# The experts' router: ranks summed by TensorE, and one lane comparison for each pick

## The reference, cut to what matters

```python
x = x + attn(layernorm(x)); x = x + xattn(layernorm(x), ctx); x = x + ffn(layernorm(x))
# ffn, xf = 2048 tokens x 256:
gates = softmax(xf @ gate_w)                       # 8 experts
topw, topi = top_k(gates, 2);  topw = topw / sum(topw)
combine = sum(topw[:, :, None] * one_hot(topi, 8), axis=1)
h = gelu(_ln(einsum('td,edh->teh', xf, w1) + b1, ln1_g, ln1_b))
y = einsum('teh,ehd->ted', h, w2) + b2
out = _ln(einsum('ted,te->td', y, combine) + xf, ln_g, ln_b)
```

## Time and profile before

| what | value |
|---|---|
| median of 3 runs | 1327.8 us (1324.22 to 1328.14) |
| the profiled execution: its time, its span | 1325.4 us, 1323.6 us |
| TensorE, VectorE, ScalarE, GpSimd busy | 91%, 73%, 47%, 24% of the span |
| mean granted TensorE clock | 0.972 of full speed |
| router, from VectorE's read of the logits to the first gather | 1079.81 to 1105.57 us |
| experts' loop and the sum behind it | 1105.57 us to the end |

### The profile page before, as it was taken

One profiled execution on the slowest core, in us unless ns is written; L12 is line 12 of the kernel. 1 busy time (PEld: TensorE's weight loads), 2 busy tenths in 40 slices (PEclk: granted clock), 3 DMA queues, 4 the chain that ended last, 5 costly groups with the idle time before them and its releaser, 6 DMA issues. The chain is left out here.

```text
span 1323.6 us, 19479 instructions
## 1 busy us (share of the span) xinstructions
PE 1206.1 (91%) x6678; PEld 734.0 (55%) x6679; DVE 972.5 (73%) x1757; ACT 622.8 (47%) x1169; POOL 321.6 (24%) x275
## 2 busy tenths in 40 slices
PE   6699999999999999969999999999999844999976
PEld 5377777887788778743333334334333232666654
DVE  3788868877887688687768777876889545677746
ACT  4233343333333333216667766776777721444432
POOL 1422235222522122112200210120000312566640
PEclk8899999999999999999999999999999986999999
DMA  7000015000400000013720570074050161111125
GB/s 260 0 7 1 1 43 106 1 1 0 75 1 1 0 1 1 1 54 56 151 37 7 96 144 0 7 131 85 1 195 1 48 158 46 60 60 63 61 82 159
DMA packets 61888, 72.99 MB, mean 55 GB/s; under 512 B 14336, under 2 KB 53376, under 8 KB 61168
## 3 DMA queue, kind: packets, MB, share of 16 engines
q1 hardware_dynamic: 55712, 59.46, 19.4%
q0 software_dynamic: 3792, 10.36, 2.5%
q10 hardware_dynamic: 2304, 2.10, 0.5%
HBM read 52.86 MB, written 18.78 MB: 54 GB/s over the span
## 5 line engine op out<-in xcount | busy, mean ns | idle before, releaser
L1512 ACT ACTIVATE pt<-pR 128x512 f32<-128x512 f32 x512 | 287.8, 600 | 102.1 <-PE pR L1399 95.9
L1607 DVE TENSOR_REDUCE neg_max<-pS 128x1 f32<-128x1024 f32 x240 | 288.1, 1220 | 63.5 <-PE pS L1377 62.0
L1399 PE MATMUL pR<-qs,ks 100*128 100x512 bf16 x512 | 187.8, 385 | 3.9 <-DVE qs L1582 2.4
L1377 PE MATMUL pS<-ks,qs 100*128 100x512 bf16 x480 | 144.9, 384 | 8.0 <-DVE neg_max L1607 6.3
L1411 PE MATMUL b_pO<-pt,b_v 128*32 128x512 f32 x1024 | 138.0, 611 | 2.3 <-ACT pt L1512 1.8
L1399 PEld LDWEIGHTS pR<-qs,ks 100*128 100x128 bf16 x512 | 49.2, 98 | 150.0 <-ACT pt L1512 44.8
L382 PE MATMUL pP<-w_feat,a_xT 128*128 128x512 f32 x256 | 123.4, 606 | 2.0 <-ACT a_xT L620 1.2
L268 POOL TENSOR_TENSOR kf<-kf,fsum 128x2048 f32<-128x2048 f32 x16 | 57.9, 3621 | 221.9 <-DVE fsum L772 221.9
L268 POOL TENSOR_TENSOR qs<-qs,fsum 128x2048 f32<-128x2048 f32 x16 | 58.8, 3674 | 150.6 <-DVE fsum L772 150.6
L440 PE MATMUL pO<-v,am 128*128 128x96 f32 x512 | 91.1, 275 | 0.0
L639 ACT COPY qfT<-pT 128x512 f32<-128x512 f32 x64 | 37.1, 580 | 108.9 <-PE pT L408 108.9
(11 more groups left out here) (321 smaller groups left out, 2190.2 us busy)
## 6 DMA issues: line engine op xcount, KB each, us to landing
ks<-k_scr SPq DMA_DIRECT2D x8, 768.0 KB
qs<-q_scr SPq DMA_DIRECT2D x24, 256.0 KB
k_scr<-f SPq DMA_DIRECT2D x18, 256.0 KB, 2.7
ks<-k_scr SPq DMA_DIRECT2D x8, 512.0 KB
ks<-in_L_ffn_w_dram SPq DMA_DIRECT2D x2, 2048.0 KB, 10.6
ks<-in_L_ffn_w_dram SPq DMA_DIRECT2D x4, 1024.0 KB, 9.6
c_y<-y_rows SPq DMA_DIRECT2D x16, 256.0 KB, 3.0
cx<-in_ctx_dram SPq DMA_DIRECT2D x3, 768.0 KB, 12.2
```

Source lines behind the costliest of these rows:

```text
L1377: ins = pe.matmul(pS1[:, slot, 512 * half:512 * half + 512], qs[0:KR, bass.ds(par, 1), h, P * t:P * t + P].rearrange("r a n -> r (a n)"), ...
L1399: pe.matmul(ring[bank], ks[0:KR, bass.ds(par, 1), h, P * j:P * j + P].rearrange("r a n -> r (a n)"), qs[0:KR, bass.ds(par, 1), h, :].rearr ...
L1512: nc.scalar.activation(pt[:, j % 2, i, :], ring[bank], ACT.Exp).then_inc(exp_done, 1)
L1607: nc.vector.tensor_reduce(neg_max[:, hg % 2, u // G, u % G:u % G + 1], pS1[:, u % 2, :], AX_X, ALU.max, negate=True).then_inc(max_done, 1)
```

## The change

- In the tail of the cross attention, two of the four `bn_stats` stand behind the first residual sum and two behind the second.
- `earlier` and `ones` get copies in bf16 (`earlier_h`, `ones_h`), cast by two more instructions ahead of the router; `both` and `lanes` become bf16. All hold whole numbers up to 127 (`both` 0 or 1).
- The copy of the logits goes; maximum and subtraction read them from PSUM.
- TensorE sums over tiles: sixteen matmuls of `ones_h` with 8 columns each, accumulated in `pT[1]`, give the totals of the experts; then one with `earlier_h` and fifteen with `ones_h`, over 120, 112, ... 8 columns, accumulated in `pT[0]`, give each tile's ranks with all earlier tiles in them. VectorE's copy and prefix sums go, and its three rank sums become one.
- `numbers` is formed ahead of `at_lane`, and `at_lane` by 32 instructions of 128 elements, each comparing the bf16 lanes with one number per partition. Each raises `hot_ready`, and each of TensorE's 32 matmuls waits for its own.
- The table of experts by slot is formed behind `from_now`.

```diff
--- before.py
+++ after.py
@@ -1726,9 +1726,10 @@
                 n = batch(B - 1, steps_before(B - 1), False, True, own)
                 for q, (kind, i, bank, _done) in enumerate(FINISH):
                     small(B - 1, kind, i, n + q, own, bank)
-                wait(dve, emptied, n + len(FINISH))
-                for t in range(T - TB, T):
-                    own.did(nc.vector.bn_stats(stats[:, t, :], xr[:, t, :]))
+                    if kind == "y":
+                        wait(dve, emptied, n + q + 1)
+                        for t in range(T - TB + 2 * i, T - TB + 2 * i + 2):
+                            own.did(nc.vector.bn_stats(stats[:, t, :], xr[:, t, :]))
 
 
 
@@ -1779,15 +1780,16 @@
         g2 = sb("g2", [P, T, E_])
         eq = sb("eq", [P, T, E_])
         sel = sb("sel", [P, 2, T, E_])
-        both = sb("both", [P, T, E_])
+        both = sb("both", [P, T, E_], BF16)
         rank = sb("rank", [P, T, E_])
-        tot = sb("tot", [P, 2, T, E_])
+        earlier_h = sb("earlier_h", [P, P], BF16)
+        ones_h = sb("ones_h", [P, P], BF16)
         order = sb("order", [P, E_])
         order_i = sb("order_i", [P, E_], I32)
         slot_i = sb("slot_i", [P, SLOTS], I32)
         slot = sb("slot", [P, SLOTS])
         lanes_i = sb("lanes_i", [P, P], I32)
-        lanes = sb("lanes", [P, P])
+        lanes = sb("lanes", [P, P], BF16)
         of_tile_i = sb("of_tile_i", [P, PICKS], I32)
         of_tile = sb("of_tile", [P, PICKS])
         of_lane_i = sb("of_lane_i", [P, PICKS], I32)
@@ -2012,13 +2014,20 @@
                     ins = pe.transpose(pH[1][:, P * c:P * c + P], lgT[:, P * c:P * c + P], ident[:, :])
                 ins.then_inc(lg_steps, 1)
                 pe.wait_ge(g_steps, 3)
-                pe.wait_ge(s_k, 7)
                 sel_2d = both[:, :, :].rearrange("p t e -> p (t e)")
-                pe.matmul(pT[0][:, 0:TE], earlier[:, :], sel_2d, start=True, stop=True).then_inc(rank_done, 1)
-                pe.matmul(pT[1][:, 0:TE], ones[:, :], sel_2d, start=True, stop=True).then_inc(rank_done, 1)
-
-                pe.wait_ge(hot_ready, 1)
+                for t in range(T):
+                    ins = pe.matmul(pT[1][:, 0:E_], ones_h[:, :], sel_2d[:, E_ * t:E_ * t + E_],
+                                    start=(t == 0), stop=(t == T - 1))
+                ins.then_inc(rank_done, 1)
+                pe.matmul(pT[0][:, 0:TE], earlier_h[:, :], sel_2d, start=True, stop=False)
+                for t in range(1, T):
+                    ins = pe.matmul(pT[0][:, E_ * t:TE], ones_h[:, :], sel_2d[:, 0:TE - E_ * t],
+                                    start=False, stop=(t == T - 1))
+                ins.then_inc(rank_done, 1)
+
+                pe.wait_ge(g_steps, 4)
                 for n in range(PICKS):
+                    wait(pe, hot_ready, n + 1)
                     ins = pe.matmul(pT[0][:, 0:2 * SLOTS], at_lane[:, n, :], numbers[:, n, :],
                                     start=(n == 0), stop=(n == PICKS - 1))
                 ins.then_inc(pairs_done, 1)
@@ -2182,16 +2191,16 @@
                 dve.wait_ge(s_k, 13)
                 own.did(nc.vector.tensor_copy(order[:, :], order_i[:, :]))
                 for to, what in ((slot, slot_i), (lanes, lanes_i), (of_tile, of_tile_i), (of_lane, of_lane_i),
-                                 (spare, spare_i)):
+                                 (spare, spare_i), (earlier_h, earlier), (ones_h, ones)):
                     own.did(nc.vector.tensor_copy(to[:, :], what[:, :]))
 
 
                 dve.wait_ge(lg_steps, 3)
-                did(nc.vector.tensor_copy(
-                    g1[:, :, :].rearrange("p (q c) e -> p c q e", q=B),
-                    pH[1][:, :].rearrange("p (c q e) -> p c q e", c=TB, q=B)[:, :, :, 0:E_]))
-                did(nc.vector.tensor_reduce(tmp[:, :], g1[:, :, :], AX_X, ALU.max))
-                nc.vector.tensor_tensor(g1[:, :, :], g1[:, :, :], tmp[:, :].unsqueeze(2).broadcast_to([P, T, E_]),
+                logits = pH[1][:, :].rearrange("p (c q e) -> p q c e", c=TB, q=B)[:, :, :, 0:E_]
+                tmp_4d = tmp[:, :].rearrange("p (q c) -> p q c", q=B)
+                did(nc.vector.tensor_reduce(tmp_4d, logits, AX_X, ALU.max))
+                nc.vector.tensor_tensor(g1[:, :, :].rearrange("p (q c) e -> p q c e", q=B), logits,
+                                        tmp_4d.unsqueeze(3).broadcast_to([P, B, TB, E_]),
                                         ALU.subtract).then_inc(g_steps, 1)
                 dve.wait_ge(g_steps, 2)
 
@@ -2217,17 +2226,8 @@
                 own.did(nc.vector.tensor_tensor(top[:, :, :], top[:, :, :],
                                                 tmp[:, :].unsqueeze(1).broadcast_to([P, 2, T]), ALU.mult))
 
-                dve.wait_ge(rank_done, 2)
-                did(nc.vector.tensor_copy(tot[:, 0].rearrange("p t e -> p (t e)"), pT[1][:, 0:TE]))
-                cur = 0
-                for step in (1, 2, 4, 8):
-                    nc.vector.tensor_copy(tot[:, 1 - cur, 0:step, :], tot[:, cur, 0:step, :])
-                    did(nc.vector.tensor_tensor(tot[:, 1 - cur, step:T, :], tot[:, cur, step:T, :],
-                                                tot[:, cur, 0:T - step, :], ALU.add))
-                    cur = 1 - cur
-                total = tot[:, cur]
-
-                did(nc.vector.tensor_scalar(tiles_i[:, :], total[:, T - 1, :], float(P - 1), None, ALU.add))
+                dve.wait_ge(rank_done, 1)
+                did(nc.vector.tensor_scalar(tiles_i[:, :], pT[1][:, 0:E_], float(P - 1), None, ALU.add))
                 did(nc.vector.tensor_scalar(tiles_i[:, :], tiles_i[:, :], 7, None, ALU.logical_shift_right))
                 own.did(nc.vector.tensor_copy(n_e[:, :], tiles_i[:, :]))
                 did(nc.vector.tensor_copy(ends[:, 0, :], tiles_i[:, :]))
@@ -2241,11 +2241,9 @@
 
                 did(nc.vector.tensor_tensor(y_base[:, :], end, n_e[:, :], ALU.subtract))
                 did(nc.vector.tensor_scalar(y_base[:, :], y_base[:, :], float(P), None, ALU.mult))
-                own.did(nc.vector.tensor_tensor(rank[:, 0, :], pT[0][:, 0:E_], y_base[:, :], ALU.add))
-                did(nc.vector.tensor_tensor(rank[:, 1:T, :].rearrange("p t e -> p (t e)"), pT[0][:, E_:TE],
-                                            total[:, 0:T - 1, :].rearrange("p t e -> p (t e)"), ALU.add))
-                did(nc.vector.tensor_tensor(rank[:, 1:T, :], rank[:, 1:T, :],
-                                            y_base[:, :].unsqueeze(1).broadcast_to([P, T - 1, E_]), ALU.add))
+                dve.wait_ge(rank_done, 2)
+                did(nc.vector.tensor_tensor(rank[:, :, :], pT[0][:, 0:TE].rearrange("p (t e) -> p t e", t=T),
+                                            y_base[:, :].unsqueeze(1).broadcast_to([P, T, E_]), ALU.add))
                 for c in range(2):
                     did(nc.vector.tensor_tensor(eq[:, :, :], sel[:, c], rank[:, :, :], ALU.mult))
                     did(nc.vector.tensor_reduce(pos[:, c, :], eq[:, :, :], AX_X, ALU.add))
@@ -2257,20 +2255,15 @@
 
                 own.did(nc.vector.tensor_tensor(at_tile, hi_2d.unsqueeze(2).broadcast_to([P, PICKS, SLOTS]),
                                                 slot[:, :].unsqueeze(1).broadcast_to([P, PICKS, SLOTS]), ALU.is_equal))
-                own.did(nc.vector.tensor_tensor(at_lane, lo_2d.unsqueeze(2).broadcast_to([P, PICKS, P]),
-                                                lanes[:, :].unsqueeze(1).broadcast_to([P, PICKS, P]), ALU.is_equal))
                 own.wait()
-                own.did(nc.vector.tensor_tensor(numbers[:, :, 0:SLOTS], at_tile,
-                                                of_tile[:, :].unsqueeze(2).broadcast_to([P, PICKS, SLOTS]), ALU.mult))
-                own.wait()
+                nc.vector.tensor_tensor(numbers[:, :, 0:SLOTS], at_tile,
+                                        of_tile[:, :].unsqueeze(2).broadcast_to([P, PICKS, SLOTS]), ALU.mult)
                 nc.vector.tensor_tensor(numbers[:, :, SLOTS:2 * SLOTS], at_tile,
                                         of_lane[:, :].unsqueeze(2).broadcast_to([P, PICKS, SLOTS]), ALU.mult
-                                        ).then_inc(hot_ready, 1)
-
-                did(nc.vector.tensor_tensor(over[:, :, :], slot[:, :].unsqueeze(2).broadcast_to([P, SLOTS, E_]),
-                                            end.unsqueeze(1).broadcast_to([P, SLOTS, E_]), ALU.is_ge))
-                did(nc.vector.tensor_reduce(s_exp[:, :], over[:, :, :], AX_X, ALU.add))
-                nc.vector.tensor_scalar(s_tab[:, :], s_exp[:, :], float(E_ - 1), None, ALU.min).then_inc(tab_ready, 1)
+                                        ).then_inc(g_steps, 1)
+                for n in range(PICKS):
+                    nc.vector.tensor_scalar(at_lane[:, n, :], lanes[:, :], lo_2d[:, n:n + 1], None, ALU.is_equal
+                                            ).then_inc(hot_ready, 1)
 
                 dve.wait_ge(pairs_done, 1)
```

(5 more changed lines are left out.)

## The result

The changed kernel took 1318.58 us, the median of four runs (1316.2 to 1318.69). The kernel before, run beside it on the same chip, took 1326.28 us (1324.22 to 1328.14). The ratio is 0.9945, with a 95% interval of 0.9927 to 0.9964: faster by 7.7 us. Forecast were 1322.1 us and a saving of 4.3 us. The profiled execution took 1316.2 us with a span of 1314.5 us, 9.1 us less than the 1323.6 us before.

A forecast was written before the change was run, and what follows sets the result against it. VectorE's own sequence in the router, with TensorE and GpSimd waiting, was taken as the bound. Savings of 0.65 + 0.32 + 2.21 + 1.08, say 4.3 us, from 1326.4 gave 1322.1 us; 1318.0 to 1326.5 should hold 8 in 10.

The forecast's parts named there:

- L to G: Router, from the logits' first read to the first gather: 25.76 us before; a saving of 3.6 us was forecast.
- late next: Gathers and first expert after the maps: most of the wait stays; the clock's rise could move the span -0.6 to +0.2.
- The statistics: Block change: two of four bn_stats move into VectorE's idle time ahead of the second residual sum, -0.65 us.
- The logits' copy: Router's start: the copy goes and VectorE reads PSUM at no added cost, -0.32 us.
- the single rank sum: Router's ranks: three rank sums on VectorE become one of 128 elements, saving 0.38 us.
- The ranks: Router: TensorE sums over tiles at 0.066 us a pair; tiles 1.83 us sooner, -2.21 us with the rank sum.
- Rival C: Rank matmuls: narrow weight loads don't overlap, 0.145 us a pair; ranks save 0.44, the whole 2.5. Chance 8%.
- The lane comparison: Slot maps: 32 comparisons 0.17 us apart with TensorE's 2.31 us of pairs beneath them, -1.08 us.
- Rival A: Lane comparison: one element at a time, 0.26 us each; the part loses 1.76, the whole saves 1.4. Chance 8%.
- rival D: Lane comparison: short comparisons cheaper, down to 0.065 us; saves 4.3 there and 7.5 in all. Chance 12%.
- Rival B: Slot maps: TensorE can't follow, 0.46 us a pair; a loss of 8.1, the whole slower by 4.9. Chance 6%.
- The check I gave for the end: From the first gather on: the forecast is wrong if this differs by over 1 us from 218 us.

The follow-up runs named there:

- experiment 2: The kernel before with only the statistics pulled forward: second residual sum to next block 1.80 us, not 2.45; single time 1328.51 us.
- Experiment 3: The changed kernel with both groups of rank matmuls on float32 operands: logits' first read to first gather 32.66 us against 21.24.
- experiment 7: The changed kernel with the totals' matmuls behind the wide rank matmuls: tiles 1.92 us after the sum of both choices, not 0.97.
- experiment 5: The changed kernel with the lanes in float32: comparisons 0.196 us apart, slots' comparison to copy of the pairs 11.03 us against 9.97.
- experiment 10: The changed kernel with picks innermost in slot map and products, lanes compared in fours, inputs bf16: 1320.86 us over 9 runs, ratio to before 0.9947.
- Experiment 6: The changed kernel with TensorE waiting for all 32 comparisons before its first pair: slots' comparison to copy of the pairs 12.10 us.
- Experiment 9: The changed kernel, unchanged, run again: 1320.83 us over 11 runs against 1326.79 for the kernel before, ratio 0.9951.
- experiment 1: The kernel before, unchanged, run again: 1325.9 us over 10 runs against 1329.97 over 13, ratio 0.9979.

## Why the prediction was right

**The mechanism.** A microsecond off VectorE's sequence in the router was a microsecond off the span: L to G fell by 4.52 us, where 3.6 were forecast, and what follows did not change (217.94 and 218.00). What the prediction called late next moved too, without effect on the total: against the first gather the clock rose 1.2 us later and an expert's first four matmuls took 0.50 us longer, but from that gather to the end the difference is 0.06 us.

**The statistics** were worth 0.65 as forecast; experiment 2 shows it alone. **The logits' copy** was worth 0.33, **the single rank sum** 0.38, both as forecast; these are read from the traces and were not tried alone.

**The ranks** are the one term mis-sized by more than a quarter of a microsecond: 2.48, not 1.83. I took a pair of 80 columns, 0.066 us, for one of 8 columns; it measures 0.028. The tiles started at 1080.69, 0.09 us after VectorE's own small steps ended: TensorE had all but caught up with them. The row I went by was, as the prediction said, filled by its columns, and could only be an upper bound. Of the two rules set beside it, on the page "TensorE: Matmul & The Clock Gate" of the Trainium skill, section "Wait — 56ns, not 53.3ns?", the floor near 25 ns agrees with the trace's 0.028 us and the 62 ns do not. Whether the matmul or its weight load sets the 0.028 is not shown. Rival C falls with it: a load lasts 0.104 us, and the next pair starts 0.028 us later all the same. (C's own working counted one load too many: by the formula of its neighbours tiles would start at 1087.50 and the ranks would save 0.60, not 0.44.) Experiment 3 shows that this holds in bf16 only, and experiment 7 that the order of the groups is worth 0.95 of it.

**The lane comparison** gave 1.32, not 1.08, since a comparison starts every 0.163 us and not every 0.17. The scaling from 512 to 128 elements was sound: on experiment 5's assumption the pitch is 0.13 us fixed and 0.26 ns per element, where I had 0.147 and 0.22. Rival A (0.26 each) and rival D (under 0.13) both fall. On the Trainium skill's page "VectorE: DVE Perf Modes", section "The TRN2 errata", the estimate was 0.094 us; the measured 0.163 decides. Of its section "The perf-mode tier table" (one-input operations run at 4x in bf16 and 2x in fp32, two-input ones at 2x and 1x) the traces bear out the direction: 0.163 against 0.196 in experiment 5, 0.83 against 1.49 in experiment 10.

**TensorE follows.** Rival B, the slower side, falls: 0.34 us from VectorE's last comparison to the copy, where it wanted 32 pairs of 0.46. Experiment 6 shows how much hung on it, 2.13 us, and also that a wait already met holds nothing up, as the prediction assumed.

**What was not foreseen** is the scatter. The forecast started from 1326.4 and assumed 2 us to either side; 19 runs of before lay between 1320.2 and 1332.2. Of the 7.7 us between the medians the traces give 5.1 to the change. That the measured time still lay in the stated range, 0.6 us above its lower end of 1318.0, owes something to luck: the forecast's own 3.0 to 5.6 us hold the 5.1 of the traces, not the 7.7 of the times.

Where the other 2.6 us come from is only in part shown. Experiment 9 shows that the early stretch of one kernel can lie 4.4 us apart, with TensorE 10 us longer at 1.2 GHz; what sets that dwell is open. But that the rest is chance alone is argued, not shown. In experiment 9's runs the mean granted clock was 0.968 or less in 11 of 19 runs of before, whose times average 1328.8 us (the other 8: 1324.6), and in none of the 11 of after (1320.3). A part of this is the change itself: around the router TensorE stood at 1.2 GHz for 30.7 and 34.1 us in before's two traces and for 27.3 in both of after's. Whether the shorter waits also keep the clock up elsewhere no run here tests; two traces of each kernel are too few to tell.

The check I gave for the end (off by over 1 us means wrong) was too tight for the same reason: experiment 1 misses it with nothing changed.

## What to carry to other kernels

When an engine waits for a whole product, cut it and let the next engine follow piece by piece, but work out both sums first: here the cut made VectorE's own part longer, and only TensorE's 2.3 us beneath it paid for that. Small sums over tiles were nearly free on TensorE in bf16 (0.028 us a pair of 8 columns) and dear in float32 (0.43). A change of a few microseconds is read from the stretch it touches, since the time of a whole run moves as much by itself.

## What the runs showed of the hardware

- A bf16 pair of weight load and 8 columns starts every 0.028 us, at 1.2 GHz, though load and matmul last 0.104 and 0.168 us; the float32 pair takes two passes of 0.214 us.
- Matmul columns read at a step of 64 bytes put pairs of 80 columns 0.138 us apart, at a step of 8 bytes about 0.076, and side by side 0.066, all at 1.2 GHz. Weights read at a step of 8 bytes cost nothing that shows.
- The same matmuls, from the first one to the second residual sum, took 1053.8 to 1062.7 us over fourteen traces, and TensorE's time at 1.2 GHz in it ran from 20.5 to 41.0 us. The shortest stretch has the least of it, but beyond that the two are not strictly in step (37.5 us with 1060.52 and 1062.65).
- TensorE's weight load starts 0.05 us after the comparison that it waits for has ended; thirty-two such waits cost nothing beyond that, and 32 waits already met left the pairs 0.066 us apart (experiment 6).
- The stretch from the experts' first bn_aggr to the logits took 10.08, 11.0 to 11.2 or 11.82 us with TensorE at 1.2 GHz for 0, 3.4 or 6.8 us of it.
